# A two-layer cross-attention kernel: weight rings, GELU copy and unit order changed in its MLP part

## The reference, cut to what matters

```python
def _L0(tgt, memory, Wq, Wk, Wv):          # no norms, no output projection
    q, k, v = heads(tgt @ Wq.T), heads(memory @ Wk.T), heads(memory @ Wv.T)
    att = merge(softmax(q @ k.T / sqrt(dk)) @ v)
    return tgt + att[0]                     # batch 0's attention, added to every batch
def _L1(x, y, ...):
    q = heads(layer_norm(x, gq, bq) @ Wq); k, v = heads(layer_norm(y, gkv, bkv) @ Wkv)
    o = merge(softmax(q @ k.T * SCALE) @ v)
    x = x + o @ Wproj + bproj
    h = gelu(layer_norm(x, gm, bm) @ W1 + b1)      # 512 -> 2048
    return x + h @ W2 + b2                          # 2048 -> 512
```

## Time and profile before

| what | us |
|---|---|
| median of 3 runs (1991.49 to 1996.76) | 1991.66 |
| profiled execution, its own time | 2001.36 |
| its span | 1999.4 |
| pass 1 / pass 2 (ticks 0 to 63 of each) | 154.1 / 166.6 |
| each of passes 3 to 8 | 184.9 to 186.9 |
| end (from `base[9]` on) | 197.7 |

### The profile page before, as it was taken

How to read it: one execution, slowest core, us unless ns; L and a number is a source line. 1 busy time by engine, 2 the same in 40 slices (tenths; PEclk the granted TensorE clock), 3 DMA queues, 4 the chain that set the end, 5 groups by cost and what they waited for, 6 DMA issues and landing times.

```text
span 1999.4 us, 23652 instructions
## 1 busy us (share of the span) xinstructions
PE 1796.6 (90%) x7488; PEld 1361.1 (68%) x7488; DVE 1165.2 (58%) x2004; ACT 1165.1 (58%) x1922; POOL 749.9 (38%) x625
## 2 busy tenths in 40 slices
PE   7899898989978989989999899899899989999888
PEld 5677676766655766767666677667676767667676
DVE  4566564678856646655665576467556555663322
ACT  3767664678856647654755575466547654764120
POOL 0355421345534334333434343343334343343221
PEclk9999999999989989999999899899999999999898
DMA  6699964556626644654465456536645554555233
GB/s 230 231 319 356 353 212 148 199 189 202 209 87 166 174 144 119 201 165 131 140 177 169 119 165 201 168 96 198 199 125 148 168 169 137 146 163 190 105 134 140
DMA packets 156379, 354.67 MB, mean 177 GB/s; under 512 B 28512, under 2 KB 47072, under 8 KB 155360
## 3 DMA queue, kind: packets, MB, share of 16 engines
q1 hardware_dynamic: 119392, 218.92, 35.6%
q10 hardware_dynamic: 36864, 134.23, 20.9%
HBM read 251.51 MB, written 82.08 MB: 167 GB/s over the span
## 4 chain that ended last, share of the span: by engine, by line
PE 56%; DMA 10%; ACT 9%; issue 8%; SPq 6%; POOL 5%; DVE 5%; ACTq 0%; DVEq 0%; POOLq 0%
PE ps_d L802 39%; PE ps_o L851 8%; DMA w_r<-w_scratch 6%; PE ps_t L834 4%; PE ps_s L819 4%; DMA q_st<-negmax_t 3%; SPq L591 2%; SPq L596 2%; ACT ps_t L955 2%; POOL p_lo L1196 1%; ACT p_hi L949 1%; PE ps_d L732 1%; ACT ps_d L867 1%; DVE negmax L1089 1%; ACT ht L925 1%
## 5 line engine op out<-in xcount | busy, mean ns | idle before, releaser
L949 ACT ACTIVATE p_hi<-ps_t 128x512 fp32r<-128x512 f32 x576 | 345.1, 599 | 524.0 <-PE ps_t L834 521.8
L1102 DVE TENSOR_TENSOR p_lo<-ps_t,p_hi 128x512 fp32r<-128x512 f32 x432 | 297.5, 689 | 338.9 <-ACT ps_t L955 336.5
L802 PE MATMUL ps_d<-w_r,g_s 128*128 128x512 f32 x1536 | 419.4, 412 | 42.7 <-DMA w_r<-w_scratch 42.7
L1196 POOL TENSOR_TENSOR p_lo<-p_full,p_hi 128x512 fp32r<-128x512 f32 x144 | 185.8, 1290 | 698.2 <-ACT p_full L955 698.0
L802 PE MATMUL ps_d<-hT,w_r 128*128 128x512 f32 x1536 | 432.1, 399 | 7.2 <-DMA w_r<-w_scratch 6.5
L1089 DVE TENSOR_REDUCE negmax<-ps_s 128x1 fp32r<-128x512 f32 x576 | 388.7, 677 | 80.0 <-PE ps_s L819 79.8
L802 PEld LDWEIGHTS ps_d<-w_r,g_s 128*128 128x128 f32 x1536 | 305.9, 200 | 124.8 <-DMA w_r<-w_scratch 47.1
L802 PEld LDWEIGHTS ps_d<-hT,w_r 128*128 128x128 f32 x1536 | 293.7, 192 | 85.2 <-issue 7.3
L834 PE MATMUL ps_t<-q_st,k_st 97*128 97x512 f32 x576 | 240.6, 418 | 52.0 <-DMA q_st<-negmax_t 31.4
L955 ACT ACTIVATE ps_t<-ps_t 128x512 f32<-128x512 f32 x432 | 257.9, 597 | 0.0
L851 PE MATMUL ps_o<-p_hi,v_s 128*65 128x512 f32 x576 | 237.9, 413 | 18.3 <-ACT o_raw L969 15.4
(11 more groups left out here) (98 smaller groups left out, 2189.7 us busy)
## 6 DMA issues: line engine op xcount, KB each, us to landing
w_r<-w_scratch ACTq DMA_DIRECT2D x256, 512.0 KB, 5.2
v_scratch<-v_out SPq DMA_DIRECT2D x36, 520.0 KB, 4.2
v_s<-v_scratch SPq DMA_DIRECT2D x36, 520.0 KB, 3.7
k_scratch<-kq_out SPq DMA_DIRECT2D x36, 512.0 KB, 5.3
q_scratch<-kq_out SPq DMA_DIRECT2D x36, 512.0 KB, 3.0
q_st<-q_scratch SPq DMA_DIRECT2D x144, 128.0 KB, 3.5
k_st<-k_scratch SPq DMA_DIRECT2D x144, 128.0 KB, 3.9
o_ab<-o_raw SPq DMA_DIRECT2D x144, 128.0 KB, 3.1
```

The costliest lines, as they stand in the source:

```text
L802: ins = nc.tensor.matmul(bank(u), lhs[a], rhs[b], start=(i == 0 and m == 0), stop=(i == 3 and m == 2))
L949: act.activation(p_hi[:, c], ps_t[:, c % 2], ACT.Exp, scale=SCALE)
L1102: dve.tensor_tensor(p_lo[:, c], ps_t[:, c % 2], p_hi[:, c].bitcast(F32), ALU.subtract).then_inc(p_split, 1)
L1196: pool.tensor_tensor(p_lo[:, POOL_CHUNK], p_full[:], p_hi[:, POOL_CHUNK].bitcast(F32), ALU.subtract).then_inc(p_pool_split, 1)
```

## The change

- The W2 ring has 6 pieces, W1's stays at 4. Loads are placed by the tick in which their first use starts (`starts`): a W1 piece 6 ticks ahead, the W2 pieces of a group 12, 10, 8 and 6 ticks ahead, never before the slot is free (`freed_by`: with six slots, pieces 0 and 1 of a group follow the group before the last one, 2 and 3 the last one). In the end SP issues them (`LATE_W_LOADS`), each after the unit that frees it.
- `h_st` has one buffer: DVE's evacuation of a hidden chunk waits for POOL's low part of the same chunk of the group before. `y2` units wait for their chunks one at a time.
- `out` waits for each joined group of heads instead of all four, and is spread over ticks 15 to 21. The bursts are at 5, 24, 40 and 55. The norm's root (POOL) stays in the tick in which the last `out` unit is out, the scaling comes one tick later (23); the output's store follows at tick 46 instead of 48.
- The end is reordered: GELU by single chunks, `y2` units of batch 7 moved between the last joins, `out` and `ht`.
- Pass 0 splits only the 8 pieces of W1 (five ticks apart), pass 1 those of W2. `Wproj` is split in four chunks just before pass 2, the bias is added in four chunks, the first residual is loaded 40 ticks earlier. In the gap, the last `tg` unit comes after 4 whole projection units instead of 6, and the gap has one tick more. Six queries' units (instead of two) are held back for pass 2.

```diff
-        for i, units in enumerate(([("tg", 0, g) for g in range(G - 1)] + late[:8], [("tg", 0, G - 1)],
-                                   late[8:11], late[11:14],
+        for i, units in enumerate(([("tg", 0, g) for g in range(G - 1)] + late[:2], late[2:6], [("tg", 0, G - 1)],
+                                   late[6:11], late[11:14],
                                    [u for pair in zip(first, late[14:18]) for u in pair], [("q", 1, 0)],
...
-        self.base = {n: gap + 7 + (n - 1) * CH for n in range(1, NP + 1)}
+        self.base = {n: gap + 8 + (n - 1) * CH for n in range(1, NP + 1)}
...
-        spread(range(base[1], base[2] + 14), queries[:-2])
+        spread(range(base[1], base[2] + 15), queries[:-6])
...
             if tail:
+                spread([at + 5], second(old, 1)[:2], front=True)
+                spread([at + 6], second(old, 1)[2:], front=True)
+                burst(at + 7, old, 2, hidden(old, 3))
                 drain = at + WEIGH
-                burst(at + 5, old, 2, second(old, 1))
-                spread([at + 6], hidden(old, 3), behind=True)
-                burst(drain, old, 3, second(old, 2))
-                spread([drain + 1], outs, front=True)
-                spread([drain + 2], second(old, 3), front=True)
-                spread([drain + 3], turns, front=True)
-                spread([drain + 4], hidden(new, 0), front=True)
-                burst(drain + 5, new, 0, hidden(new, 1))
-                burst(drain + 6, new, 1, second(new, 0))
-                spread([drain + 7], hidden(new, 2), front=True)
-                burst(drain + 8, new, 2, second(new, 1))
-                spread([drain + 9], hidden(new, 3), front=True)
-                burst(drain + 10, new, 3, second(new, 2))
-                spread([drain + 11], second(new, 3), front=True)
-                self.ticks = drain + 13
+                spread([drain - 1], second(old, 2)[:2], behind=True)
+                by_chunk(drain - 1, old, 3)
+                spread([drain + 1], second(old, 2)[2:], front=True)
+                spread([drain + 2], second(old, 3)[:1], front=True)
+                spread([drain + 3], outs, front=True)
+                spread([drain + 4], second(old, 3)[1:3], front=True)
+                spread([drain + 5], turns[:2] + second(old, 3)[3:] + turns[2:], front=True)
+                spread([drain + 6], hidden(new, 0), front=True)
+                by_chunk(drain + 6, new, 0)
+                spread([drain + 7], hidden(new, 1), front=True)
+                by_chunk(drain + 7, new, 1)
+                spread([drain + 8], second(new, 0), front=True)
+                spread([drain + 9], hidden(new, 2), front=True)
+                by_chunk(drain + 9, new, 2)
+                spread([drain + 10], second(new, 1), front=True)
+                spread([drain + 11], hidden(new, 3), front=True)
+                by_chunk(drain + 11, new, 3)
+                spread([drain + 12], second(new, 2), front=True)
+                spread([drain + 13], second(new, 3), front=True)
+                self.ticks = drain + 15
                 continue
             if old:
                 burst(at + 5, old, 2, second(old, 1)[:2])
-                spread(range(at + 6, at + 14), second(old, 1)[2:] + hidden(old, 3)[:2])
-                spread(range(at + 14, at + 23), outs + hidden(old, 3)[2:])
-                burst(at + 23, old, 3, second(old, 2)[:2])
+                spread(range(at + 6, at + 15), second(old, 1)[2:] + hidden(old, 3)[:3])
+                spread(range(at + 15, at + 22), outs)
+                spread(range(at + 22, at + 24), hidden(old, 3)[3:])
+                burst(at + 24, old, 3, second(old, 2)[:2])
                 rest = second(old, 2)[2:]
-                spread(range(at + 24, at + 42), turns[:1] + rest[:1] + turns[1:2] + rest[1:] + turns[2:] + hidden(new, 0))
-                burst(at + 42, new, 0, second(old, 3)[:2])
-                spread(range(at + 43, at + 56), second(old, 3)[2:] + hidden(new, 1))
+                spread(range(at + 25, at + 40), rest[:1] + turns[:2] + rest[1:] + turns[2:] + hidden(new, 0))
+                burst(at + 40, new, 0, second(old, 3)[:2])
+                spread(range(at + 41, at + 55), second(old, 3)[2:] + hidden(new, 1))
             else:
-                spread(range(at + 14, at + 23), outs[:1] + queries[-2:-1] + outs[1:3] + queries[-1:] + outs[3:])
-                spread(range(at + 25, at + 42), turns + hidden(new, 0))
-                burst(at + 42, new, 0, [])
-                spread(range(at + 43, at + 56), hidden(new, 1))
-            burst(at + 56, new, 1, second(new, 0)[:2])
-            spread(range(at + 57, at + CH + 5), second(new, 0)[2:] + hidden(new, 2))
+                spread(range(at + 15, at + 22), outs)
+                spread(range(at + 22, at + 35), queries[-6:])
+                spread(range(at + 35, at + 44), turns + hidden(new, 0))
+                burst(at + 44, new, 0, [])
+                spread(range(at + 45, at + 55), hidden(new, 1))
+            burst(at + 55, new, 1, second(new, 0)[:2])
+            spread(range(at + 56, at + CH + 5), second(new, 0)[2:] + hidden(new, 2))
...
+    at = tuple(emptied("out", i, t) for t in range(TC))
+    return at, at[-1], (at[-1] + 1,) * 4
...
-    return PRE + 19 + (i * 5) // 2
+    return PRE + 19 + 5 * i if i < PIECES // 2 else PLAN.base[1] + 4 + 5 * (i - PIECES // 2)
...
-RES_SUMS = listed([(PLAN.base[n + 1] + (10 if n == 1 else 3) + t, (n, t)) for n in range(1, NP) for t in range(TC)])
-BIAS_AT = PLAN.base[2] + 8
-WO_AT = PLAN.base[1] + 30
+RES_SUMS = listed([(PLAN.base[n + 1] + (4 if n == 1 else 3) + t, (n, t)) for n in range(1, NP) for t in range(TC)])
+BIAS_AT = PLAN.base[2] + 2
+WO_AT = PLAN.base[1] + 48
...
-        for c in range(HC):
-            before = n * HC + c - 4 - HC
-            freed = PLAN.end("hid", before // HC + 1, before % HC) + 1 if before >= 0 else PLAN.base[1] + 56
-            first.append((max(freed, PLAN.base[n + 1] - 8), (n, c)))
-        for group in range(4):
-            before = n * 4 + group - 1 - 4
-            at = PLAN.base[2] + 30
-            if before >= 0:
-                at = PLAN.end("y2", before // 4 + 1, before % 4 * 4 + 3) + 1
-            second += [(at + (2 * c if at < PLAN.base[NP] else 0), (n, group, c)) for c in range(4)]
...
+        res.append((PLAN.base[n + 1] - (40 if n == 1 else 0), n))
...
+W1_RING, W2_RING = 4, 6
+W1_PIECES = [(n, c) for n in range(1, NP) for c in range(HC)]
+
+
+def freed_by(kind, j):
+    if kind == "w1":
+        return ("hid", *W1_PIECES[j - W1_RING]) if j >= W1_RING else None
+    if j < W2_RING:
+        return None
+    n, c = W1_PIECES[j - W2_RING]
+    return ("y2", n, c // 4 * 4 + TC - 1)
+
+
+def weight_tables():
+    early, late = [], []
+    for j, (n, c) in enumerate(W1_PIECES):
+        for kind in ("w1", "w2"):
+            u = freed_by(kind, j)
+            freed = PLAN.end(*u) + 1 if u else 0
+            if kind == "w1":
+                at = PLAN.starts["hid", n, c] - 6
+            else:
+                at = PLAN.starts["y2", n, c // 4 * 4] - 12 + 2 * (c % 4)
+            at = max(freed, at)
+            if at < PLAN.base[NP]:
+                early.append((at, (kind, j)))
+            else:
+                late.append((NO[u], PLAN.end(*u), (kind, j)))
+    return listed(early), listed([(at, x) for _, at, x in sorted(late)])
...
-    h_st = sb("h_st", [P, 2, 4, T], F32)
+    h_st = sb("h_st", [P, 4, T], F32)
+    w2_at = place[0]
+    w2_r = sb("w2_r", [P, W2_RING, 2, D], F32R)
     w1_at = place[0]
-    w1_r = sb("w1_r", [P, 4, FC, 2, P], F32R)
-    w2_at = place[0]
-    w2_r = sb("w2_r", [P, 4, 2, D], F32R)
+    w1_r = sb("w1_r", [P, W1_RING, FC, 2, P], F32R)
...
+            elif i in (PIECES // 2, PIECES // 2 + 1):
+                sp.wait_ge(unit_ready, ready("a", 10, FC - 1))
...
-                if c == 0 and i == 0:
-                    pe.wait_ge(o_joined, (n + 1) * G)
+                if c == 0:
+                    pe.wait_ge(o_joined, n * G + i + 1)
                     if n == 1:
-                        pe.wait_ge(wo_split, 1)
+                        pe.wait_ge(wo_split, i + 1)
...
-                    if i == 0:
-                        pe.wait_ge(g_split, done + 1)
-                    pe.wait_ge(w2_loaded[i], 16 * ((n - 1) * 4 + group + 1))
+                    pe.wait_ge(g_lo, 4 * done + i + 1)
+                    pe.wait_ge(w2_loaded[j % W2_RING], 16 * (j // W2_RING + 1))
...
+        def load_weight(kind, j):
+            u = freed_by(kind, j)
+            if u:
+                act.wait_ge(unit_ready, ready(*u))
...
-                act.activation(h_st[:, done % 2], h_st[:, done % 2], ACT.Gelu).then_inc(gelu_done, 1)
+                act.activation(h_st[:], h_st[:], ACT.Gelu).then_inc(gelu_done, 4)
...
-                if c == 0:
-                    act.wait_ge(gelu_done, done + 1)
```

(46 more changed lines are left out.)

120 lines of the change are left out of this document (64 added, 56 removed).

## The result

| | before | after |
|---|---|---|
| median (4 runs each) | 1991.58 us | 1890.05 us (1886.24 to 1895.5) |
| ratio, 95% interval | | 0.9486 [0.9458, 0.9515] |
| profiled execution / its span | 2001.4 / 1999.4 | 1895.5 / 1893.5 |
| mean granted clock | 0.949 | 0.970 |

A forecast was written before the change was run, and what follows sets the result against it. PE, busy for 90% of the span, was taken to set the pace. Gains of 69 (passes 3 to 8), 13 (pass 1 and 2), 6 (gap), 4 (pass 0) and 18 (end) make 110 us off 1991.7: 1882 us, range 1855 to 1905.

The forecast's parts named there:

- the waits for W at ticks 5 and 56 go: 5.7 us a pass, and 2.2 us of clock: Passes 3 to 8: earlier W2 issue ends PE's weight waits, 34.0 / 6 = 5.7 us a pass, plus 2.2 of clock.
- The step for `oT`: Passes 3 to 8: PE's wait for the last joined heads ahead of `out` goes, 3.2 and 1.6 us a pass.
- I count this as unchanged: 15.4 / 6 = 2.6 us stay: Passes 3 to 8: PE's waits for the low part of probabilities behind a burst stay at 2.6 us a pass.
- The row of maxima: Passes 3 to 8: PE's wait for this row grows from 2.5 us a pass by 1.2, bounds 0 and 6.4.
- less 2 for the W2 pieces that POOL and the queues now have there: Pass 1: splitting the W2 pieces there costs 2 us, set against a gain of 4.
- Pass 0: 4 forecast: Pass 0: half the piece traffic leaves, saving 4 of 10.2 us of waits; bounds 0 and 10.2 plus some clock.
- Gap: 6 forecast: Gap: the last `tg` no longer waits behind DVE's queued evacuations, 5.1 us and about 1 of clock.
- clock loss is 18 us now; I take 3 of it: End: of about 18 us lost to PE's lower clock, 3 us are regained.
- The row takes the place: Rival, seven passes: 5.2 MB queued make the row of maxima wait up to 6.4 us; 1910 us, chance 0.15.
- Limited by bandwidth: Rival, weight loads: earlier pieces queue too, half of 34.0 us stays with its clock; 1910 us, chance 0.1.
- The burst's pause laid bare at 5 and 40: Rival: waits hidden by the weight wait appear at these ticks, 4.8 us twice in seven passes; 1949 us, chance 0.1.
- One `h_st`: Rival, slower: POOL's late low parts hold up DVE's hidden chunks and PE; about 2010 us, chance 0.05.

The follow-up runs named there:

- experiment 3: The changed kernel with the MLP weight ring of four and the old places for W1 and W2 loads: 0.9597, 1913.25 us.
- experiment 7: The changed kernel with `out` waiting for all four joined groups at its first part: 0.9511, 1897.93 us.
- experiment 6: The changed kernel with the norm's scaling back in the root's tick, 22 instead of 23: 0.9589, 1913.11 us.
- experiment 8: The changed kernel with all 16 weight pieces split in pass 0 again, 2.5 ticks apart: 0.9466, 1887.62 us.
- experiment 9: The changed kernel with one GELU over four chunks in the end instead of four by chunk: 0.9459, 1886.44 us.
- experiments 1 to 3: The changed kernel with a W2 ring of four, with W2 pieces four ticks later, with the weight part undone: 0.9602, 0.9526, 0.9597.
- experiment 1: The changed kernel with the W2 ring of six back to four, at the new places: 0.9602, 1916.39 us.
- experiment 5: The changed kernel with the bursts of ticks 24, 40 and, in pass 2, 44 one tick later: 0.9353, 1867.11 us.
- experiment 4: The changed kernel with the output store at tick 52 instead of 46, behind the row of maxima: 0.9362, 1868.47 us.

## Why the prediction came out as it did

**Passes 3 to 8: 69 forecast, 68.6 measured, with other parts.** The step "the waits for W at ticks 5 and 56 go: 5.7 us a pass, and 2.2 us of clock" holds for the waits (34.0 to 0) but is too dear as a price of the weight part: with that part undone these passes are 2.2 us longer each, not 7.9 (experiment 3). Only 3.1 us a pass of wait for weights come back, so the other parts of the change had taken away the rest (there is none at tick 56); 1.3 us of them come off the row of maxima; and the clock stays at 0.98. The step for `oT`, 3.2 us, holds (19.3 to 0), and its cause is the later start (experiment 7). "I count this as unchanged: 15.4 / 6 = 2.6 us stay" is wrong twice over. In the kernel before, waits for the low part and for ACT's copy were 15.4 + 5.8 = 21.2 us; after, 30.3. The copy's 5.8 us are not in the prediction's list of waits. The burst directly behind the scaling made it dearer, as I had feared in the sentence before, and yet the tick between root and scaling saves more than that: without it, 42.7 us (experiment 6). The row of maxima I took at 3.7 us a pass; it is 3.3.

That the sum of a pass comes out to 0.1 us is luck: the waits gave 1.5 us less than forecast (6.2 for 7.7), and the clock about as much more. I had 3.8 us a pass for it; the waits of PE fell by 6 us, and 11.4 were gained. Before, PE was at 1.2 GHz for 17 to 20 us of each pass: behind the wait at tick 5, behind that at 14, at 25, in two passes at 55. After, it is for 3 to 10, at 25 and 51. Half of the difference of 65 us in six passes is 32 us, 5.4 a pass.

**Pass 1 and 2: 13 forecast, -4.1 measured.** The failed step is "less 2 for the W2 pieces that POOL and the queues now have there". The pieces cost pass 1 13.8 us (experiment 8: 161.9 against 148.1), seven times that, through POOL's low parts and waits behind full DMA engines, with a clock of 0.91. Without them pass 1 takes 148.1 us, 6.0 less than before, for the 4 that I took between 0 and 7.9. In pass 2 the two waits of the earlier trace rows are gone and the clock gave the 7 us taken for it (0.93 to 0.97), but PE's waits for ACT's copy, put at nothing, rose from 3.3 to 11.2 us:

```profile
PE ps_o L906 <- ACT o_raw L1023: 11.2, 4, 6.9
```

6.9 us of them are at tick 45. The burst of pass 2 has no `y2` unit as cover, neither before nor after; at tick 42 it cost 2.9 us for the low part and 0.7 for the copy, at tick 44 it stands directly ahead of the copy that `pv` of tick 45 needs. I wrote of a burst laid bare at tick 5 and not of this one. Another 3.7 us are at tick 25, where pass 2 has the norm's scaling ahead of the copy and no burst at all.

**Pass 0: 4 forecast, 13.2 measured.** The same error seen from the other side: eight pieces fewer are worth 10.4 us here (experiment 8), and the upper bound of 10.2 "plus some clock" was the better value. Forecast of pass 0, 1 and 2 together: 17; measured 9.1.

**Gap: 6 forecast, 2.8 measured.** The wait of 5.1 us behind the inversion is gone, as forecast; but the first `tg` now waits 2.7 us where it waited 1.3, a `k` unit waits 0.7 us more, and the 1 us of clock did not come: PE is at 1.2 GHz for 10.2 us of the gap in both kernels. I had not looked at the first `tg`. No run takes the parts of the gap's change apart.

**End: 18 forecast, 26.5 measured.** The three waits that I kept are there, each near its size: 2.5 for 2.3 (weights of 7.12), 3.0 for 2.9 (`ht`), 2.5 for 2.3 (last group), the end of the kernel after:

```profile
PE ps_d L857 <- DMA w_r<-w_scratch: 5.7, 4, 2.5
PE ps_d L787 <- ACT ht L977: 3.0, 1, 3.0
```

The waits fell from 22.3 to 8.7, 13.6 us for the 15 forecast. The mis-sized term is "clock loss is 18 us now; I take 3 of it": at 0.99 it is 1.7 us, so most of it went. The other 12.9 us of the 26.5 are this, where 3 stood. The weight part gives 8.5 us of the end's gain (experiment 3), GELU by chunks none (experiment 9).

**The whole.** That 1882 is near 1890 is in part luck: pass 1 and 2 fell short by 17 us, the gap by 3, and pass 0 and the end gave 9 and 8.5 us more. In passes 3 to 8 the waits that were to go did go; where work was moved between stretches, the price was wrong.

**The rivals.** *The row takes the place*: not as a rule; one pass comes near its 6.4 us (5.7), the mean of 3.3 is below the 3.7 of the forecast. *Limited by bandwidth*: not for the kernel after, whose W waits are zero; but the trade of W against row in experiments 1 to 3 is this rival's mechanism in part. The limit of 358 GB/s that it leans on is passed elsewhere in the trace (417, experiment 1). *The burst's pause laid bare at 5 and 40*: no wait above 0.6 us there in passes 3 to 8; in pass 2 it is what happened, at tick 45. *One `h_st`*: DVE waits for POOL's low part 7.4 us in the whole run, all of it in the end, none in a pass. Its price was added up wrongly: 16 us in seven passes on 1882 are 1994, not 2010. The last 4 us between forecast and median are the profiled executions: before's lay 9.7 above its median, after's 5.4.

## What to carry to other kernels

When PE waits in several places of a period, price a wait by what is late next on the same resource: here weights and the row of maxima shared the DMA engines, and waits of 3.1 us a pass for the one were worth 2.2; moving one 1 MB store behind the short transfer that PE needs was worth as much as a larger ring and a new placement. An in-order engine wants the long item (table load, GELU, table load) behind the short one that opens the next accumulation, and a wait on another engine at least a tick away from it. Work moved from one full stretch to another is moved and not saved, and goes into the sum with the price that it had where it came from.

## What the runs showed of the hardware that I had not expected

- The clock came back for more than the waits were worth: waits of PE above 2 us in passes 3 to 8 fell from four or five places in a pass to one or two, and the time at 1.2 GHz from 109 to 44 us; with the wait at tick 25 gone too (experiment 5) it is 14 us. With a wait for weights of 3 us back in every pass (experiment 3) it stayed at 41. Which of the waits of before pulled the clock down each time is not settled by these runs.
- Behind a store of 1 MB on the same queue the next loads took 1.36, 1.41 and 1.02 us to issue, against 0.5 to 0.6 us without it (experiment 4). It is not always so: in pass 5 of experiment 1, with the store in the same place, they took 0.78, 0.58 and 0.49 us.
- The row of maxima, a small transfer, was there 5.2 us after its last issue behind the store, and 9.5 us after it with more weights around it (experiment 1).
- Engines that are full do not move the same everywhere: at a DMA share of 1.0 the traces have 417 GB/s at the start of the kernel and 318 around the store.
- No drain stands around the table loads of the kernel after (starts 1092.87, 1094.80, with 1.92 us of GELU between), against the 1.38 us that the Trainium skill states for each (page "ScalarE: Activation LUTs", What ACT_TABLE_LOAD costs); the measurement decides.
